# Dividing local probabilities before they are turned, instead of scaling the attention output by turned inverses

## The chip, the cores and the metric

The kernel runs on one core of a Trainium2 chip. The metric is the device time of one execution in microseconds. Before the change the median of three runs is 2158.35 us (2157.47 to 2159.66). The engines named below are PE (TensorE: matrix products and transposes), ACT (ScalarE), DVE (VectorE), POOL (GpSimd) and SP (the engine that issues most DMAs). Each takes its instructions strictly in program order and waits on semaphores where another engine has to be first.

## The reference, cut to what matters

The input is four sequences of 1024 tokens with 256 features. A first sublayer is causal attention with 16 heads of 16 features. The second part, in which the change lies, is two layers of local attention with a gated feed-forward, over the same four sequences:

```python
for l in range(2):                        # 8 heads of 64 features, windows of 128 tokens
    h = shift_token(x)
    q, k, v = split(h @ wqkv)
    q = l2norm(q) * q_scale ; k = l2norm(k) * k_scale
    q, k = rotary_xpos(q, k)
    # window w of queries looks at the keys of windows w-1 and w
    sim  = einsum('bhwid,bhwjd->bhwij', q * 8, k)        # 128 queries x 256 keys
    sim  = where(mask, -big, sim)
    attn = softmax(sim, axis=-1)
    x = x + einsum('bhwij,bhwjd->bhwid', attn, v) @ wo
    h = layernorm(shift_token(x)) * ln_g + ln_b
    a, g = split(h @ w1 + b1)
    x = x + (a * gelu(g)) @ w2 + b2
```

The softmax is exp(sim - max) divided by its sum over the keys. The sum belongs to one query of one head, so the division may be made on the 256 probabilities of each query and head, or after the product with v, on its 64 output features.

## The kernel before, in words

The block `layers` takes from about 740 us to the end. It runs eight iterations, `it` = 0 to 7: one layer of one sequence each, four for layer 0 and four for layer 1. An iteration is `attention(it)` and then `feed_forward(it, more)`, which also makes the first windows of the next iteration. The order on each engine is written out by hand.

`attention` counts steps u = 0 to 31 and some more. A window `w` = u // 4 has 128 tokens (`NT` = 8 windows), and a unit u is one window and two of its eight heads; `p` = u % 4. A unit goes through these stations:

- PE `scores` (L1414) writes the scores of two units, u and u+1 for even u, to the PSUM banks `s_ps`.
- DVE `mask_scores` (L1948) adds the band, takes the maximum and writes to `p_sb`, four operations of 128x256 for two units. `p_sb` is a ring of four units.
- ACT `exponentials` (L1680), two operations per unit, makes the exponentials in place in `p_sb` and leaves their sums in `total`. In step u stands unit u.
- PE `turn_probs` (L1485) transposes unit u-2 in step u into `pt_ps`, ACT `copy_probs` (L1702) copies it out, PE `values` (L1510) multiplies two units by v into `o_ps`.
- ACT `copy_output` (L1718) copies a finished window from `o_ps` to `o_t`, where features stand in the partitions and tokens in the free dimension.

The probabilities in `p_sb` are not normalised. DVE inverts the eight sums of a window in `invert_sums` (L2000). ACT spreads each inverse over 64 columns into `inv_wide` in `widen_sums` (L1711). PE transposes that with four transposes in `spread_sums` (L1494) into the bank `turn_ps`. DVE multiplies `o_t` by it in `scale_output` (L2006), and then `project_out` (L1430) may use it.

Between these stand the stations that prepare later windows, in the same queues. For window w+3: PE `project` (L1368), ACT `square` (L1643), DVE `sums` (L1919, at p = 3), POOL `norms` (a clamp, L1831, and a power, L1833). For window w+2: DVE `unit_vectors` (L1925, at p = 0) multiplies q and k by the inverse norms, DVE `times_sin` (L1939, at p = 1, four operations of 128x256) and POOL `rotate` (L1841 twice, then the addition L1846) turn them. DVE `low_x` (L1913, at p = 2) and ACT `high_x` (L1657) split the input of window w+4. PE `turn` (L1394) transposes q and k of window w+1 into `turn_ps`, ACT copies them out (L1672). `unit_vectors` and `times_sin` run for window indices w = 1 to 5, so five times in the `attention` of an iteration; `sums` runs there for w = 0 to 4.

In the trace `p_sb`, `qn`, `rot_c`, `squares`, `inv_wide` and `gate` are all called x_all, since they lie in that tile's memory.

## Time and profile before

| what | before |
|---|---|
| median of three runs | 2158.35 us |
| the profiled execution: its own time | 2157.21 us |
| its span | 2155.4 us |
| PE busy | 1973.2 us (92%) |
| DVE busy | 1466.5 us (68%) |
| ACT busy | 1260.7 us (58%) |
| POOL busy | 756.0 us (35%) |
| PE clock granted, mean share of full speed | 0.972 |

The profiled execution takes 1.8 us more than its span, and 1.1 us less than the median of the runs. The share of an engine's busy time is a mean over stages with quite different limits. The stretch of the change repeats in every iteration, so it is read from the order of time within one iteration.

### The profile page before, as it was taken

To read this page: it belongs to the slowest core of one execution; us is meant where nothing else is said; L and a number is where in the kernel's file an instruction comes from. 1 tells how busy PE (TensorE), PEld (TensorE's weight loads), DVE (VectorE), ACT (ScalarE), POOL (GpSimd) and SP (SyncE) were. 2 spreads that over 40 slices of the span, in tenths; PEclk is the share of its full clock that TensorE was granted. 3 is DMA by queue.
4 is the path that set the end of the run, shared out by engine and by line. 5 is a ranking of instruction groups with operands and counts; after the bars stand their busy time and mean duration, and the time that the engine had idled before them with its cause. 6 is when DMAs were issued, how large, how long until landed. Compare 5 with 4: busy or idle time off the path is not lost.

```text
span 2155.4 us, 36296 instructions
## 1 busy us (share of the span) xinstructions
PE 1973.2 (92%) x12096; PEld 1247.4 (58%) x12096; DVE 1466.5 (68%) x3928; ACT 1260.7 (58%) x3012; POOL 756.0 (35%) x631
## 2 busy tenths in 40 slices
PE   7978999999897669999999999999999999999998
PEld 4522333333234446777777676676777677777766
DVE  7778888888863557568568567557757756856854
ACT  4526666666664337647547646645755764754763
POOL 1033121121322456056046136236515605614610
PEclk9969999999999879999999999999999999999999
DMA  6667534535315620000000000023001000000000
GB/s 182 165 115 148 68 47 61 69 53 93 72 59 144 183 83 1 21 20 1 21 15 6 21 11 11 4 78 113 2 20 40 2 21 30 11 21 21 21 1 30
DMA packets 105335, 112.21 MB, mean 52 GB/s; under 512 B 49772, under 2 KB 84160, under 8 KB 104128
## 3 DMA queue, kind: packets, MB, share of 16 engines
q1 hardware_dynamic: 104576, 100.97, 20.6%
q0 software_dynamic: 576, 8.91, 1.1%
q8 instruction: 100, 1.64, 0.3%
q14 instruction: 83, 0.68, 0.1%
HBM read 67.12 MB, written 42.47 MB: 51 GB/s over the span
## 4 chain that ended last, share of the span: by engine, by line
PE 47%; DVE 6%; ACT 5%; issue 3%; POOL 3%; DVEq 0%; ACTq 0%; POOLq 0%
PE qkv_ps L1368 11%; PE s_ps L1414 5%; PE pt_ps L1485 5%; PE s_ps L1472 4%; PE o_ps L1510 3%; PE qkv_ps L1430 3%; PE pt_ps L1555 3%; POOL inv_norm L1833 2%; PE o_ps L1472 2%; PE pt_ps L1472 2%; PE s_ps L1430 2%; PE o_ps L1555 2%; ACT x_all L1680 2%; PE turn_ps L1394 2%; PE turn_ps L1494 1%
## 5 line engine op out<-in xcount | busy, mean ns | idle before, releaser
L689 ACT ACTIVATE probs<-st_ps 128x512 f32<-128x512 f32 (+3 forms) x768 | 330.0, 495 | 165.5 <-PE st_ps L594 164.9
L1368 PE MATMUL qkv_ps<-w_qkv,x_parts 128*128 128x512 f32 x1152 | 311.8, 415 | 25.6 <-DVE x_all L1925 18.8
L579 PE MATMUL s_ps<-k_stack,q_stack 96*128 96x512 bf16 (+3 forms) x768 | 242.6, 347 | 36.5 <-DVE piece_negmax L734 25.6
L734 DVE CUSTOM_DVE_ANT_0 att_in<-s_ps,causal 128x128 f32<-128x128 f32 (+3 forms) x512 | 233.7, 484 | 42.1 <-PE s_ps L579 41.9
L1368 PEld LDWEIGHTS qkv_ps<-w_qkv,x_parts 128*128 128x128 f32 x1152 | 214.3, 195 | 79.9 <-issue 30.0
L1680 ACT ACTIVATE x_all<-x_all,negmax 128x256 f32<-128x256 f32 (+1 forms) x512 | 249.4, 491 | 8.2 <-DVE negmax L1948 7.8
L1948 DVE CUSTOM_DVE_ANT_0 x_all<-s_ps,band 128x256 f32<-128x256 f32 (+1 forms) x512 | 178.3, 402 | 110.5 <-PE s_ps L1414 110.0
L594 PE MATMUL st_ps<-q_stack,k_stack 98*128 98x512 bf16 (+3 forms) x768 | 241.2, 335 | 12.3 <-ACT probs L689 10.1
L1702 ACT COPY att_in<-pt_ps 128x512 f32<-128x512 f32 (+1 forms) x256 | 143.0, 559 | 147.3 <-PE pt_ps L1485 145.9
L816 POOL TENSOR_SCALAR_AFFINE_SELECT probs<-probs 128x512 f32<-128x512 f32 x128 | 81.2, 634 | 414.7 <-ACT probs L689 414.7
L1841 POOL TENSOR_TENSOR x_all<-x_all,turn_by 128x512 f32<-128x512 f32 x128 | 179.9, 1425 | 101.4 <-PE turn_ps L1394 56.4
L1939 DVE TENSOR_TENSOR rot_s<-x_all,turn_by 128x256 f32<-128x256 f32 x256 | 207.3, 870 | 0.3
L737 DVE TENSOR_REDUCE piece_negmax<-s_ps 128x1 f32<-128x512 f32 x256 | 175.9, 687 | 29.3 <-PE s_ps L579 28.9
L1833 POOL TENSOR_TENSOR inv_norm<-sum_sq,neg_half 128x16 f32<-128x16 f32 x64 | 187.5, 2930 | 5.3
L1846 POOL TENSOR_TENSOR x_all<-x_all,rot_s 128x1024 f32<-128x1024 f32 x64 | 157.1, 2455 | 48.6 <-DVE rot_s L1939 48.5
L611 PE MATMUL o_ps<-probs,v_all 128*32 128x512 f32 (+3 forms) x1536 | 166.1, 505 | 1.2 <-POOL probs L816 0.7
L1485 PE MATMUL pt_ps<-ident,x_all 128*128 128x128 f32 x960 | 160.5, 287 | 6.9 <-ACT att_in L1702 6.9
L594 PEld LDWEIGHTS st_ps<-q_stack,k_stack 98*128 98x128 bf16 x768 | 72.1, 98 | 159.4 <-ACT probs L689 124.4
L579 PEld LDWEIGHTS s_ps<-k_stack,q_stack 96*128 96x128 bf16 x768 | 75.7, 99 | 149.4 <-DVE piece_negmax L734 71.4
L1414 PE MATMUL s_ps<-k_t,q_t 64*128 64x256 f32 (+1 forms) x1152 | 139.9, 366 | 0.8 <-DVE negmax L1948 0.8
L1485 PEld LDWEIGHTS pt_ps<-ident,x_all 128*128 128x128 f32 x960 | 101.4, 141 | 66.4 <-issue 59.3
L1472 PE MATMUL s_ps<-hn_t,w_ffn 128*128 128x512 f32 (+1 forms) x528 | 133.5, 400 | 0.0
(148 smaller groups left out, 3410.6 us busy)
## 6 DMA issues: line engine op xcount, KB each, us to landing
qk_scratch<-parts SPq DMA_DIRECT2D x64, 192.0 KB, 2.8
q_stack<-qk_scratch SPq DMA_DIRECT2D x96, 128.0 KB, 6.5
k_stack<-qk_scratch SPq DMA_DIRECT2D x96, 128.0 KB, 7.0
w_ffn<-ffn_weights POOLq DMA_DIRECT2D x4, 2176.0 KB, 11.5
x_in<-xt_scratch SPq DMA_DIRECT2D x16, 512.0 KB, 4.1
ffn_weights<-w_high SPq DMA_DIRECT2D x2, 2176.0 KB, 7.5
ffn_weights<-w_raw SPq DMA_DIRECT2D x2, 2176.0 KB, 13.1
att_scratch<-att SPq DMA_DIRECT2D x32, 128.0 KB, 2.0
```

What stands on the lines that cost most here:

```text
L579: pe.matmul(s_ps[i % 3][:, 0:kw], q_stack[0:STK, slot, h, qt * P:(qt + 1) * P], k_stack[0:STK, slot, h, k0:k0 + kw], start=True, stop=True ...
L594: pe.matmul(st_ps[i % 3][:, q0:CH], k_stack[0:STK + SHIFT, slot, h, kt * P:(kt + 1) * P], q_stack[0:STK + SHIFT, slot, h, c * CH + q0:(c + ...
L689: act.activation(probs[:, n % 3, h, q0:CH], st_ps[i % 3][:, q0:CH], ACT.Exp).then_inc(exp_done.sem, 1)
L734: dve.tensor_tensor_reduce(seen[:, i % 3, 0:kw], s_ps[i % 3][:, 0:kw], causal[:, CH - kw:CH], -1.0, BIG, ALU.add, ALU.min, result).then_in ...
L1368: mm = pe.matmul(qkv_ps[:, part * CH:(part + 1) * CH], x_parts[:, w % XR, xp, k, :], w_qkv[:, wp, k, part * INNER:(part + 1) * INNER], sta ...
L1414: mm = pe.matmul(s_ps[side][:, to:to + (t1 - t0) * P], q_t[r, w % 2, p, :], k_t[r, p, t0 % KR * P:(t0 % KR + t1 - t0) * P], start=True, st ...
L1472: mm = pe.matmul(up_pair(c, j)[bank][0:rows, :], w_up(w, k, tile)[:, 0:rows], hn_t[:, h, k, :], start=n == 0, stop=n == len(steps) - 1)
L1485: mm = pe.transpose(pt_ps[:, (h * 2 + kt) * P:(h * 2 + kt + 1) * P], p_sb[:, u % 4, h, kt * P:(kt + 1) * P], ident[:, :])
L1680: act.activation(p_sb[:, u % 4, h, k0:PW], p_sb[:, u % 4, h, k0:PW], ACT.Exp, scale=-1.0, bias=negmax[:, u % 4, h:h + 1], accum_out=total[ ...
L1833: pool.tensor_tensor(inv_norm[:, :], sum_sq[:, 1, :], neg_half[:, 0:2 * H2], ALU.pow)\
L1841: ins = pool.tensor_tensor(heads(rot_c, j), heads(qn, j), turn_by[:, w, 2 * j, :].unsqueeze(1) .to_broadcast([P, H2, HD2]), ALU.mult)
L1939: dve.tensor_tensor(dst[:, :, o], src[:, :, i], turn_by[:, w, 2 * j + 1, o].unsqueeze(1) .to_broadcast([P, H2, half]), ALU.mult).then_inc( ...
```

## The change

The probabilities of a unit are normalised before they are transposed. DVE gets a function `divide(u)`: a reciprocal of the unit's two sums (128x2) and a multiplication of the unit's probabilities in `p_sb` (128x512, 128x256 in window 0) by it, in place. The second waits for the first by a semaphore. At the end of each odd step DVE divides units u-1 and u. `turn_probs` waits for the division instead of the exponentials. `invert_sums`, `widen_sums`, `spread_sums` and `scale_output` are gone with their semaphores, and `project_out` waits for `copy_output` alone. ACT makes the exponentials of two units in succession in the even step, four operations, where it made two in each step. `total` and `inv_total` are a ring of four units.

```diff
-        total = sb("total", [P, 2, PAIRS, 2])
-        inv_total = sb("inv_total", [P, 2, PAIRS, 2])
+        total = sb("total", [P, 4, 2])
+        inv_total = sb("inv_total", [P, 4, 2])
...
-        inv_sum = count("inv_sum", NT, 2)
-        widened = count("widened", NT)
-        spread = count("spread", NT)
-        o_scaled = count("o_scaled", NT)
+        inv_sum = count("inv_sum", UNITS)
+        divided = count("divided", UNITS)
...
-                if w >= 3 and j == 0:
-                    pe.wait_ge(o_scaled.sem, o_scaled.of(it, w - 3))
...
-                pe.wait_ge(o_scaled.sem, o_scaled.of(it, t1 // P - 1))
+                pe.wait_ge(o_copied.sem, o_copied.of(it, t1 // P - 1))
...
-                    pe.wait_ge(exp_done.sem, exp_done.of(it, 2 * u + 1))
+                    pe.wait_ge(divided.sem, divided.of(it, u))
...
-                def spread_sums(w):
-                    pe.wait_ge(widened.sem, widened.of(it, w))
-                    pe.wait_ge(turn_copied.sem, turn_copied.of(it, 2 * min(w + 2, NT - 1) + 1))
-                    for p in range(PAIRS):
-                        mm = pe.transpose(turn_ps[:, p * P:(p + 1) * P], inv_wide[:, 2 * p:2 * p + 2, :], ident[:, :])
-                    mm.then_inc(spread.sem, 1)
...
-                    if u >= PAIRS + 2 and (u - 2) % PAIRS == 0:
-                        spread_sums((u - 2) // PAIRS - 1)
...
             def exponentials(it, u):
                 w, k0 = u // PAIRS, 0 if u // PAIRS else WIN
-                if u % PAIRS == 0:
-                    act.wait_ge(inv_sum.sem, inv_sum.of(it, w - 2))
                 for h in range(2):
                     act.wait_ge(s_masked.sem, s_masked.of(it, 2 * u + h))
                     act.activation(p_sb[:, u % 4, h, k0:PW], p_sb[:, u % 4, h, k0:PW], ACT.Exp, scale=-1.0,
                                    bias=negmax[:, u % 4, h:h + 1],
-                                   accum_out=total[:, w % 2, place(u, h)[0], place(u, h)[1]:place(u, h)[1] + 1]).then_inc(exp_done.sem, 1)
+                                   accum_out=total[:, u % 4, h:h + 1]).then_inc(exp_done.sem, 1)
...
-                def widen_sums(w):
-                    act.wait_ge(inv_sum.sem, inv_sum.of(it, w))
-                    if w:
-                        act.wait_ge(spread.sem, spread.of(it, w - 1))
-                    act.copy(inv_wide[:, :, :], inv_total[:, w % 2].rearrange("p a s -> p (a s)").unsqueeze(2)
-                             .to_broadcast([P, H2, HD2])).then_inc(widened.sem, 1)
...
-                    if EARLY <= u < UNITS:
+                    if EARLY <= u < UNITS and u % 2 == 0:
                         exponentials(it, u)
+                        exponentials(it, u + 1)
...
-                    if u >= PAIRS + 1 and (u - 1) % PAIRS == 0:
-                        widen_sums((u - 1) // PAIRS - 1)
...
-                def invert_sums(w):
-                    dve.wait_ge(exp_done.sem, exp_done.of(it, 2 * (w + 1) * PAIRS - 1))
-                    if w >= 2:
-                        dve.wait_ge(widened.sem, widened.of(it, w - 2))
-                    dve.reciprocal(inv_total[:, w % 2], total[:, w % 2]).then_inc(inv_sum.sem, 1)
-                def scale_output(w):
-                    dve.wait_ge(spread.sem, spread.of(it, w))
-                    dve.wait_ge(o_copied.sem, o_copied.of(it, w))
-                    window = o_t[:, :, w % WPC * P:(w % WPC + 1) * P]
-                    dve.tensor_tensor(window, turn_ps[:, :].rearrange("p (h t) -> p h t", h=PAIRS), window, ALU.mult)\
-                       .then_inc(o_scaled.sem, 1)
+                def divide(u):
+                    k0 = 0 if u // PAIRS else WIN
+                    dve.wait_ge(exp_done.sem, exp_done.of(it, 2 * u + 1))
+                    dve.reciprocal(inv_total[:, u % 4], total[:, u % 4]).then_inc(inv_sum.sem, 1)
+                    dve.wait_ge(inv_sum.sem, inv_sum.of(it, u))
+                    probs = p_sb[:, u % 4, :, k0:PW]
+                    dve.tensor_tensor(probs, probs, inv_total[:, u % 4, :].unsqueeze(2).to_broadcast([P, 2, PW - k0]),
+                                      ALU.mult).then_inc(divided.sem, 1)
...
-                    if u >= PAIRS + 1 and (u - 1) % PAIRS == 0:
-                        invert_sums((u - 1) // PAIRS - 1)
-                    if u >= PAIRS + 3 and (u - 3) % PAIRS == 0:
-                        scale_output((u - 3) // PAIRS - 1)
...
                     if p == 1 and 0 < w < NT - 2:
                         times_sin(it, w + 2)
+                    if u % 2 and u < UNITS:
+                        divide(u - 1)
+                        divide(u)
```

The first engine is DVE, at the place where `unit_vectors` and `times_sin` of a window stand (steps p = 0 and 1), before and after the change. An ISA row with x_all and s_ps is a mask operation, the ISA row behind it is the read-out of its maximum.

```order
L1925 TENSOR_TENSOR x_all<-qkv_ps,inv_norm 128x1024
L2000 RECIPROCAL inv_total<-total 128x8
L1939 TENSOR_TENSOR rot_s<-x_all,turn_by 128x8x32 x4
L1948 ISA x_all,negmax<-s_ps,band 128x256
L1948 ISA negmax 128x1
```

```order
L1899 TENSOR_TENSOR x_all<-qkv_ps,inv_norm 128x1024
L1913 TENSOR_TENSOR rot_s<-x_all,turn_by 128x8x32 x4
L1973 RECIPROCAL inv_total<-total 128x2
L1976 TENSOR_TENSOR x_all<-x_all,inv_total 128x512
L1973 RECIPROCAL inv_total<-total 128x2
L1976 TENSOR_TENSOR x_all<-x_all,inv_total 128x512
L1922 ISA x_all,negmax2<-s2_ps0,band 128x256
L1922 ISA negmax2 128x1
```

Two divisions now stand between `times_sin` and the masks of the next two units.

The next place on DVE is the end of the same window (p = 2 and 3), from `low_x` to the masks that follow, before and after.

```order
L1913 TENSOR_TENSOR x_parts<-x_in,x_parts 128x256
L1919 TENSOR_REDUCE sum_sq<-x_all 128x16
L2006 TENSOR_TENSOR o_t<-turn_ps,o_t 128x4x128
L1948 ISA x_all,negmax<-s_ps,band 128x256
L1948 ISA negmax 128x1
```

```order
L1887 TENSOR_TENSOR x_parts<-x_in,x_parts 128x256
L1893 TENSOR_REDUCE sum_sq<-x_all 128x16
L1973 RECIPROCAL inv_total<-total 128x2
L1976 TENSOR_TENSOR x_all<-x_all,inv_total 128x512
L1973 RECIPROCAL inv_total<-total 128x2
L1976 TENSOR_TENSOR x_all<-x_all,inv_total 128x512
L1922 ISA x_all,negmax2<-s2_ps0,band 128x256
L1922 ISA negmax2 128x1
```

The scaling of the output is gone and two divisions stand behind `sums`.

On ACT, from `copy_probs` at p = 2 to the next `copy_probs` but one; the ACTIVATE rows into x_all and total are the exponentials, the one from qkv_ps is `square`.

```order
L1702 COPY att_in<-pt_ps 128x512
L1680 ACTIVATE x_all,total<-x_all,negmax 128x256 x2
L1643 ACTIVATE x_all<-qkv_ps 128x1024
L1718 COPY o_t<-o_ps 128x4x128
L1702 COPY att_in<-pt_ps 128x512
L1680 ACTIVATE x_all,total<-x_all,negmax 128x256 x2
```

```order
L1685 COPY att_in<-pt_ps 128x512
L1663 ACTIVATE x_all,total<-x_all,negmax 128x256 x4
L1628 ACTIVATE x_all<-qkv_ps 128x1024
L1693 COPY o_t<-o_ps 128x4x128
L1685 COPY att_in<-pt_ps 128x512
L1650 COPY v_tok<-qkv_ps 128x512
```

`square` now stands behind four exponentials instead of two.

## Rows read from the trace of the kernel before

**Rows 1.** The page, busy time, share of the span and instructions of each engine.
```profile
PE 1973.2 (92%) x12096; PEld 1247.4 (58%) x12096; DVE 1466.5 (68%) x3928; ACT 1260.7 (58%) x3012; POOL 756.0 (35%) x631
```
**Rows 2.** Stretches: length, busy PE, PEld, DVE, ACT, POOL (instructions), granted clock, DMA.
```profile
1140.00:1189.50 49.50, 47.44 (x376) 35.79 (x376) 42.28 (x100) 38.33 (x102) 33.55 (x20) 1.00 0.01 2
...
690.00:700.00 10.00, 6.79 (x37) 4.98 (x38) 6.01 (x23) 2.68 (x9) 3.94 (x10) 1.00 0.88 265
...
750.00:760.00 10.00, 0.00 (x0) 0.00 (x0) 5.57 (x7) 0.46 (x1) 7.17 (x5) 0.73 0.00 0
760.00:770.00 10.00, 7.90 (x26) 6.25 (x26) 0.00 (x0) 2.15 (x3) 1.28 (x1) 0.58 0.01 2
```
**Rows 3.** Timeline of DVE, fourth iteration: start, duration, line, operands, [idle before].
```profile
1152.34 1.23 DVE L1925 TENSOR_TENSOR x_all<-qkv_ps,inv_norm 128x1024 f32<-128x1024 f32 x1 [0.30 <-POOL inv_norm L1833]
1153.48 0.19 DVE L2000 RECIPROCAL inv_total<-total 128x8 f32<-128x8 f32 x1
1153.60 3.61 DVE L1939 TENSOR_TENSOR rot_s<-x_all,turn_by 128x256 f32<-128x256 f32 x4
1157.13 0.41 DVE L1948 CUSTOM_DVE_ANT_0 x_all<-s_ps,band 128x256 f32<-128x256 f32 x1
...
1158.50 1.52 DVE L1913 TENSOR_TENSOR x_parts<-x_in,x_parts 128x256 fp32r<-128x256 f32 x1
1159.95 1.21 DVE L1919 TENSOR_REDUCE sum_sq<-x_all 128x16 f32<-128x1024 f32 x1
...
1164.65 1.23 DVE L1925 TENSOR_TENSOR x_all<-qkv_ps,inv_norm 128x1024 f32<-128x1024 f32 x1
...
1189.45 1.22 DVE L1925 TENSOR_TENSOR x_all<-qkv_ps,inv_norm 128x1024 f32<-128x1024 f32 x1
```
**Rows 4.** Timeline of POOL in the same window.
```profile
1157.35 2.39 POOL L1846 TENSOR_TENSOR x_all<-x_all,rot_s 128x1024 f32<-128x1024 f32 x1 [0.76 <-DVE rot_s L1939]
1161.35 0.25 POOL L1831 TENSOR_SCALAR sum_sq<-sum_sq 128x16 f32<-128x16 f32 x1 [1.61 <-DVE sum_sq L1919]
1161.68 2.93 POOL L1833 TENSOR_TENSOR inv_norm<-sum_sq,neg_half 128x16 f32<-128x16 f32 x1
```
**Rows 5.** Groups of instructions by line: shapes and count | busy us, mean ns.
```profile
L1494 PE MATMUL turn_ps<-ident,x_all 128*128 128x128 f32 x256 | 38.9, 274 | 4.5 <-ACT x_all L1711 4.5
L1711 ACT COPY x_all<-inv_total 128x512 f32<-128x512 f32 x64 | 39.6, 618 | 1.4 <-DVE inv_total L2000 1.0
L2006 DVE TENSOR_TENSOR o_t<-turn_ps,o_t 128x512 f32<-128x512 f32 x64 | 43.9, 685 | 91.4 <-ACT o_t L1718 91.4
```
**Rows 6.** Timeline of DVE in the causal part: a reciprocal and the multiplication that waits for it.
```profile
166.69 0.26 DVE L759 RECIPROCAL inv_sum<-ot_ps 128x16 f32<-128x16 f32 x1 [0.64 <-PE ot_ps L619]
166.98 0.42 DVE L762 TENSOR_TENSOR att<-ot_ps,inv_sum 128x256 f32<-128x256 f32 x1
```
**Rows 7.** Timeline of DVE and POOL in a feed-forward.
```profile
1278.07 1.21 DVE L1919 TENSOR_REDUCE sum_sq<-x_all 128x16 f32<-128x1024 f32 x1
1279.20 0.68 DVE L2048 TENSOR_TENSOR hidden<-x_all,hidden 128x512 fp32r<-128x512 f32 x1
1279.48 0.51 POOL L1831 TENSOR_SCALAR sum_sq<-sum_sq 128x16 f32<-128x16 f32 x1 [7.35 <-DVE sum_sq L1919]
1280.08 2.93 POOL L1833 TENSOR_TENSOR inv_norm<-sum_sq,neg_half 128x16 f32<-128x16 f32 x1
...
1281.31 0.41 DVE L1913 TENSOR_TENSOR x_parts<-x_in,x_parts 128x256 fp32r<-128x256 f32 x1
```
**Rows 8.** Timeline of ACT in the window of rows 3.
```profile
1157.58 0.51 ACT L1680 ACTIVATE x_all<-x_all,negmax 128x256 f32<-128x256 f32 x1
...
1158.86 1.02 ACT L1643 ACTIVATE x_all<-qkv_ps 128x1024 f32<-128x1024 f32 x1 [0.19 <-PE qkv_ps L1368]
```
**Rows 9.** Timeline of PE at the end of the attention.
```profile
1225.96 0.60 PE L1494 MATMUL turn_ps<-ident,x_all 128*128 128x128 f32 x4
```
**Rows 10.** Timeline of POOL in window 0 of the iteration.
```profile
1132.20 2.40 POOL L1846 TENSOR_TENSOR x_all<-x_all,rot_s 128x1024 f32<-128x1024 f32 x1 [0.76 <-DVE rot_s L1939]
```

More of the change, by code:

```diff
@@ L1148, in layers @@
         spare = x_all[:, :, :].rearrange("p t d -> p (t d)")
-        at = list(itertools.accumulate((0, GS * CH, 8 * PW, TC * D, H2 * HD2, 2 * INNER, 2 * INNER, 2 * INNER)))
-        gate, p_sb, fin, inv_wide, squares, qn, rot_c = [spare[:, i:j] for i, j in zip(at, at[1:])]
+        at = list(itertools.accumulate((0, GS * CH, 8 * PW, TC * D, 2 * INNER, 2 * INNER, 2 * INNER)))
+        gate, p_sb, fin, squares, qn, rot_c = [spare[:, i:j] for i, j in zip(at, at[1:])]
         gate = gate.rearrange("p (j n) -> p j n", j=GS)
@@ L1153, in layers @@
         fin = fin.rearrange("p (t d) -> p t d", t=TC)
-        inv_wide = inv_wide.rearrange("p (h d) -> p h d", h=H2)
         p_t = out_in[0][:, :, :, :].rearrange("p t g n -> p (t g n)").rearrange("p (u h k t) -> p u h k t", u=4, h=2, k=2)
@@ L1897, in _ @@
         def _(dve):
-            for c in (qn_ready, sin_ready, s_masked, inv_sum, mid_ready, hn_t_split, hidden_ready, hidden_split, out_ready):
+            for c in (qn_ready, sin_ready, s_masked, mid_ready, hn_t_split, hidden_ready, hidden_split, out_ready):
                 dve.sem_inc(c.sem, c.credit)
```

## The prediction

> **What bounds the kernel now.** I read the page's busy times first. PE is busy 92% of the span [rows 1], which suggests that whatever unloads PE helps. That is a mean, so I then took the busy times of the stretch that the change touches, 1140 to 1189.5 us, in the fourth iteration. There PE is busy for 47.4 of 49.5 us, but DVE too for 42.3 us [rows 2]. A busy PE is not PE at its peak, so the busy shares don't say who sets the pace. The order of time does [rows 3, 4]. One window, from one `unit_vectors` (L1925) to the next, takes 1164.65 - 1152.34 = 12.31 us, and no step of it is a wait for PE:
>
> - `unit_vectors` and the small reciprocal: 1152.34 to 1153.60, 1.26 us
> - `times_sin`: to 1157.13, 3.53 us
> - four masks: to 1158.50, 1.37 us
> - `low_x`: to 1159.95, 1.45 us
> - from the start of `sums` to the next `unit_vectors` 4.70 us: 1.21 us of `sums` and, behind it, POOL's clamp and its power of 2.93 us.
>
> Their sum is 12.31 us, the whole period. So the loop is closed by DVE and POOL: DVE is full from `unit_vectors` to the end of `sums`, and then POOL's power is waited for, while DVE does the scaling of the output and the next masks. The reader should see that work placed between `unit_vectors` and `sums` lengthens the window one for one, and that work placed behind `sums` is covered by POOL. The three periods from 1152.34 to 1189.45 have a mean of 12.37 us [rows 3]. Five `unit_vectors` stand in the attention of an iteration, with four periods between them, and with eight iterations there are 32 periods.
>
> **What goes.** 256 transposes on PE, 64 copies on ACT, 64 multiplications on DVE, of 38.9, 39.6 and 43.9 us busy [rows 5]. Four transposes occupy PE for at most 0.60 us [rows 9]. In the loop above none of this lies on the path; only the small reciprocal does, with 1.26 - 1.14 = 0.12 us a window (1152.34 to 1153.48 is 1.14). The 91.4 us in which DVE waits for ACT's copy of the output [rows 5] look like a prize, but most of them lie where DVE has no other work due (windows 6 and 7), so I count them at nothing.
>
> **What comes.** 256 reciprocals and 256 multiplications on DVE. The pair costs: a reciprocal of eight columns 0.19 us [rows 3]; between a reciprocal and a multiplication that waits for it by a semaphore 166.98 - 166.69 - 0.26 = 0.03 us [rows 6]; and a multiplication of 128x512 with both inputs in SBUF about 0.68 us, of which 0.61 before the next starts (the nearest row is L2048 [rows 7]). Two divisions are 2 x 0.83 = 1.66 us if nothing disturbs them.
>
> Something does, at the place behind `times_sin`. POOL's addition L1846 runs there from 1157.35 for 2.39 us, and `low_x`, a DVE operation with two SBUF inputs, took 1.52 us and ended 0.28 us after it [rows 3, 4]; the same operation takes 0.41 us where POOL does not do such work [rows 7]. The masks, with one input in PSUM, were not held up. In the other direction the clamp L1831 took 0.51 instead of 0.25 us beside L2048 [rows 4, 7]. I read this as: a two-input SBUF operation of DVE and a POOL operation take turns, whole. The Trainium skill (GPSIMD Engine Reference, Key points) says that GpSimd shares its SBUF interfaces with VectorE and contends with DVE instructions that have two SBUF inputs. By that rule the multiplications here, with two SBUF inputs, are the exposed kind and the scaling that goes, with one input in PSUM, was not; the trace agrees, 1.52 against 0.41 us. Without the rule the time would be that of the first rival below.
>
> So one of the two multiplications waits for most of L1846. If POOL is first (its addition starts 0.14 us after `times_sin` ended at 1157.21): 2.4 us, then 0.61, 0.22 and 0.61 us, 3.85 us in all. If DVE is first: 0.2 + 0.65 + 2.35 + 0.6 = 3.8. I take 3.8 us; the lower bound is 1.66 and the upper 1.66 + 2.39 = 4.05.
>
> **The new period.** Both divisions stand ahead of the masks, and the masks ahead of the exponentials, and `square` now stands behind four exponentials. Step by step from `unit_vectors`:
>
> - `unit_vectors` 1.14, `times_sin` 3.53, divisions 3.8
> - first mask to first exponential 1157.58 - 1157.13 = 0.45 [rows 3, 8]
> - four exponentials of 0.51 each [rows 8], 2.03
> - `square` to `sums`: 1159.95 - 1158.86 = 1.09. Until now `square` came early enough that DVE was the later one; now `sums` waits for it some 1.8 us, since masks and an unhindered `low_x` are over after 1.37 + 0.36 = 1.7 us against 3.57
> - `sums` to the next `unit_vectors` 4.70, and 0.45 more since the clamp meets the first multiplication of the divisions behind `sums`. In rows 7 that meeting moved the power to 2.01 us after the start of `sums`, against 1.73 (0.28 more); the new multiplication starts about 0.15 us later than L2048 did there.
>
> Sum 17.19 us against 12.37, so +4.82 us a period, 32 periods: +154.2 us. The divisions behind `sums` (1.66 us) and the next four masks (1.4 us) fit into the 3.9 us that POOL takes. PE needs at most 47.4 / 4 = 11.9 us a window (the stretch of rows 2 holds four periods) and gets 17, so it waits.
>
> **The rest of an iteration.** From the last `times_sin` to the end of the attention PE was nearly full. There four `spread_sums` of 0.6 us go, 2.4 us, and the scaling with its wait goes from the end. Against this stand a chain of about 4.2 us for two units (first mask to exponential 0.45, exponentials 2.03, divisions 1.66), below the 5 us that PE takes for two units there, and 3.8 us of divisions at its beginning. I estimate -0.5 us an iteration (bounds -2.5 and +3; the -2.4 nearly used up by the longer latency of each pair of units): -4 us. In window 0 the first division meets POOL's addition of 1132.20 to 1134.6 [rows 10], and `turn_probs` and `sums` come later: about +0.5 us (0 to 2): +4 us. The feed-forward is untouched.
>
> The total is 154.2 - 4 + 4 = +154 us. The profiled execution of 2157.2 us becomes 2311.4 us. The median of the runs lies 1.1 us higher than that execution, so I predict 2312 us, 7% slower.
>
> **Rivals.**
>
> - *No turn-taking for the divisions, or much overlap.* Then they cost 1.66 instead of 3.8 us behind `times_sin`: 2.14 x 32 = 68 us less, and without the late clamp another 0.45 x 32 = 14 us less, 2230 us. If `square` too were early enough, another 1.8 us a period, 2172 us would be the floor of this family. For it: `low_x` is the only such row in the loop. Against: the two rows agree in both directions.
> - *PE's clock falls.* PE now waits in each window, so its load drops to some 12 of 17 us. At 750 to 770 us, where PE did nothing for 10 us and then started again, the granted clock was 0.73 and 0.58, a mix of its two levels of 2.4 and 1.2 GHz; with PE busy for 6.8 of 10 us at 690 to 700 us it was 1.00 [rows 2]. The new waits are at most 3 to 4 us long, so I think it holds. If it halved in a third of the time, PE's 12 us a window would become 16, still below 17, and only the PE-bound stretches of about 40 us an iteration would pay, some 5 us each: 2350 us.
> - *Faster.* If PE is what sets the pace in the loop after all, 0.6 us of PE goes for each of 64 windows, 38 us, and DVE's divisions lie in its waits: 2119 us. It decides if the end of `sums` no longer sets the next `unit_vectors`, that is, if DVE had over 5 us of slack between them. The rows show 12.31 us of closed chain, so this is unlikely.
>
> **Chances.** The forecast's mechanism (2280 to 2335 us) 0.62; the milder cases (2172 to 2280) 0.22; the clock (2335 to 2400) 0.12; faster 0.02; another slow case 0.02. A measurement of this kernel can tell about 0.2% from no change. The range leaves out the far ends on either side: 2235 to 2345 us. Faster 0.02, within 0.2% 0.02, slower 0.96.
>
> **What the changed profile would show.** The period between two `unit_vectors` is 17 us (not 12.4); one of the two multiplications behind `times_sin` has a duration near 3 us, the others near 0.68; `sums` waits for ACT's `square`; `unit_vectors` still waits for POOL's power or starts right behind it; the clamp takes 0.5 to 0.7 us; PE has idle time of about 5 us a window, most of it ahead of L1485, released by DVE. The prediction is wrong if the multiplications behind `times_sin` are all short, if the loop is closed by another chain, or if the granted clock falls below 0.9 in the attention.

## The result, and the profile after

| | before | after |
|---|---|---|
| median of the runs | 2157.91 us (2156.68 to 2159.66, 4 runs) | 2339.18 us (2337.71 to 2340.73, 4 runs) |
| the profiled execution: own time | 2157.2 us | 2340.7 us |
| its span | 2155.4 us | 2339.0 us |
| PE clock granted, mean | 0.972 | 0.955 |

The change makes the kernel 8.35% slower: the ratio is 1.0835 [1.0822, 1.0848]. The prediction was 2312 us with a range of 2235 to 2345 us, so the direction and most of the size were right; 27 us were missing. The measured time lies 4 us above the 2280 to 2335 us that the prediction gave to its own mechanism.

The page of after, busy times, against [rows 1]:

```profile
PE 1993.8 (85%) x11840; PEld 1246.1 (53%) x11840; DVE 1668.8 (71%) x4312; ACT 1222.7 (52%) x2948; POOL 817.5 (35%) x631
```

PE lost 256 transposes and is busy 20 us longer all the same: the same matrix products took longer at a lower granted clock. DVE has 202 us more. POOL has the same 631 instructions and 61 us more, which only waiting inside them can explain.

One window of the loop, the timeline of DVE in after, fourth iteration, against [rows 3]. Of four masks (L1922) the first is shown, and of the four reciprocals (L1973, 0.15 us each) none:

```profile
1204.48 1.22 DVE L1899 TENSOR_TENSOR x_all<-qkv_ps,inv_norm 128x1024 f32<-128x1024 f32 x1 [1.45 <-POOL inv_norm L1807]
1205.74 3.59 DVE L1913 TENSOR_TENSOR rot_s<-x_all,turn_by 128x256 f32<-128x256 f32 x4
...
1209.44 0.69 DVE L1976 TENSOR_TENSOR x_all<-x_all,inv_total 128x512 f32<-128x512 f32 x1
...
1210.24 2.69 DVE L1976 TENSOR_TENSOR x_all<-x_all,inv_total 128x512 f32<-128x512 f32 x1
1212.84 0.41 DVE L1922 CUSTOM_DVE_ANT_0 x_all<-s_ps,band 128x256 f32<-128x256 f32 x1
...
1214.22 0.42 DVE L1887 TENSOR_TENSOR x_parts<-x_in,x_parts 128x256 fp32r<-128x256 f32 x1
1216.32 1.22 DVE L1893 TENSOR_REDUCE sum_sq<-x_all 128x16 f32<-128x1024 f32 x1 [1.68 <-ACT x_all L1628]
...
1217.64 0.69 DVE L1976 TENSOR_TENSOR x_all<-x_all,inv_total 128x512 f32<-128x512 f32 x1
...
1218.44 0.69 DVE L1976 TENSOR_TENSOR x_all<-x_all,inv_total 128x512 f32<-128x512 f32 x1
...
1221.95 1.23 DVE L1899 TENSOR_TENSOR x_all<-qkv_ps,inv_norm 128x1024 f32<-128x1024 f32 x1 [1.45 <-POOL inv_norm L1807]
```

POOL in the same window, against [rows 4]:

```profile
1209.47 2.89 POOL L1820 TENSOR_TENSOR x_all<-x_all,rot_s 128x1024 f32<-128x1024 f32 x1 [0.76 <-DVE rot_s L1913]
1217.73 0.71 POOL L1805 TENSOR_SCALAR sum_sq<-sum_sq 128x16 f32<-128x16 f32 x1 [5.37 <-DVE sum_sq L1893]
1218.53 3.39 POOL L1807 TENSOR_TENSOR inv_norm<-sum_sq,neg_half 128x16 f32<-128x16 f32 x1
```

ACT there, against [rows 8]; between the two rows stand the other three exponentials:

```profile
1213.30 0.51 ACT L1663 ACTIVATE x_all<-x_all,negmax 128x256 f32<-128x256 f32 x1 [1.83 <-DVE negmax L1922]
...
1215.28 1.00 ACT L1628 ACTIVATE x_all<-qkv_ps 128x1024 f32<-128x1024 f32 x1
```

The period is 1221.95 - 1204.48 = 17.47 us, where 17.19 was forecast. Of the two multiplications behind `times_sin` the second takes 2.69 us. It began at 1210.24 while POOL's addition ran from 1209.47 to 1212.36, and ended 0.57 us after that addition, about the length of one multiplication. The addition itself took 2.89 instead of 2.39 us, since the first multiplication, begun 0.03 us earlier, was ahead of it. `low_x` is down from 1.52 to 0.42 us, but `sums` waits 1.68 us for `square`.

In the last three iterations of after, the first of the four periods is shorter: 15.96, 15.11 and 15.11 us. Rows of DVE and POOL from the seventh, without the reciprocals:

```profile
1973.82 1.43 DVE L1913 TENSOR_TENSOR rot_s<-x_all,turn_by 128x256 f32<-128x256 f32 x4
1974.91 3.17 POOL L1815 TENSOR_TENSOR x_all<-x_all,turn_by 128x512 f32<-128x512 f32 x2 [2.38 <-PE turn_ps L1389]
...
1975.36 1.58 DVE L1976 TENSOR_TENSOR x_all<-x_all,inv_total 128x512 f32<-128x512 f32 x1
...
1977.05 1.57 DVE L1976 TENSOR_TENSOR x_all<-x_all,inv_total 128x512 f32<-128x512 f32 x1
```

Here POOL's own multiplications (L1815) came late, waiting for PE. `times_sin` took 1.43 us without them, where it takes 3.59 us beside them, and the two divisions met them instead. So `times_sin` takes turns with POOL too, and has done so before the change: its 3.61 us in [rows 3] lie beside POOL's L1841.

Adding up the starts of `unit_vectors` over all eight iterations tells where the 183.6 us of the two spans went. The loop is the time from the fourth to the eighth `unit_vectors` of an iteration (four periods), window 0 that from the first to the fourth, and the tail that from the eighth to the first of the next iteration:

| sums in us | before | after | difference | forecast |
|---|---|---|---|---|
| loop, 32 periods | 399.5 | 553.4 | +153.9 | +154.2 |
| window 0, 8 times | 371.5 | 376.4 | +4.9 | +4 |
| tails, 7 of them | 527.5 | 547.8 | +20.3 | -3.5 |
| behind the last `unit_vectors` | 102.9 | 107.3 | +4.4 | -0.5 |

(First and last starts 753.98 and 2052.51 us before, 754.10 and 2231.74 us after.) The loop is right and the tail is wrong. Stretches of whole tails, before first and then three of after: start and end, length, busy PE, PEld, DVE, ACT, POOL (instructions), granted clock, DMA; the third row of after is 4 us out of its second tail.

```profile
1189.45:1264.12 74.67, 71.25 (x441) 51.75 (x438) 39.25 (x107) 41.68 (x96) 11.03 (x9) 1.00 0.05 19
```

```profile
1064.07:1140.29 76.22, 68.79 (x415) 49.44 (x416) 47.73 (x121) 37.87 (x86) 12.66 (x9) 1.00 0.05 18
1256.94:1334.43 77.49, 70.88 (x419) 50.88 (x419) 47.63 (x121) 37.88 (x86) 12.66 (x9) 0.98 0.05 18
1284.92:1288.92 4.00, 4.00 (x27) 2.67 (x27) 1.77 (x8) 0.50 (x2) 0.00 (x0) 0.61 0.00 0
```

In the one tail of after that is at the full clock throughout PE is busy for 2.46 us less, as forecast (2.4 us), and yet the tail is 1.55 us longer: PE's idle time grew from 3.42 to 7.43 us. In six of the seven tails of after there are in addition between one and three stretches of some 4 us at 0.57 to 0.71 of the full clock, where six of seven tails of before were at 1.00 throughout. The same place on PE in before, the waits for DVE's `hn` and ACT's copy:

```profile
1215.74 1.09 PE L1449 MATMUL qkv_ps<-ident,hn 128*128 128x128 f32 x8 [1.26 <-DVE hn L1979]
...
1221.30 0.63 PE L1485 MATMUL pt_ps<-ident,x_all 128*128 128x128 f32 x4 [0.77 <-ACT att_in L1702]
```

and in after, in the tail that holds the third row above:

```profile
1279.48 0.63 PE L1480 MATMUL pt_ps<-ident,x_all 128*128 128x128 f32 x4 [1.02 <-ACT att_in L1685]
...
1284.06 1.46 PE L1444 MATMUL qkv_ps<-ident,hn 128*128 128x128 f32 x8 [2.35 <-DVE hn L1953]
1285.45 2.08 PE L1409 MATMUL s_ps<-k_t,q_t 64*128 64x256 f32 x8
...
1292.08 0.63 PE L1480 MATMUL pt_ps<-ident,x_all 128*128 128x128 f32 x4 [2.08 <-ACT att_in L1685]
```

The scores at 1285.45 take 2.08 us, at 1277.32 they took 1.14: the two levels of the clock, 1.2 and 2.4 GHz, behind a wait of 2.35 us for DVE.

### The profile page after: what moved, and what is told of

It is laid out like the page before. It is cut to its first block, busy times and chain, and to the rows that moved or that the text cites. A ratio compares the mean times of both kernels' runs of the same rounds, so it can differ in the third digit from the quotient of the medians.

```text
span 2339.0 us, 35807 instructions
## 1 busy us (share of the span) xinstructions
PE 1993.8 (85%) x11840; PEld 1246.1 (53%) x11840; DVE 1668.8 (71%) x4312; ACT 1222.7 (52%) x2948; POOL 817.5 (35%) x631
## 4 chain that ended last, share of the span: by engine, by line
PE 30%; DVE 16%; ACT 8%; POOL 8%; issue 6%; DVEq 0%; POOLq 0%; ACTq 0%
POOL inv_norm L1807 6%; DVE rot_s L1913 6%; PE qkv_ps L1365 4%; ACT x_all L1663 4%; PE s_ps L1467 4%; PE qkv_ps L1425 3%; PE pt_ps L1480 3%; DVE sum_sq L1893 3%; PE pt_ps L1540 2%; DVE x_all L1899 2%; PE s_ps L1409 2%; PE o_ps L1467 2%; PE pt_ps L1467 2%; PE o_ps L1540 2%; PE s_ps L1425 2%
## 5 line engine op out<-in xcount | busy, mean ns | idle before, releaser
L1480 PE MATMUL pt_ps<-ident,x_all 128*128 128x128 f32 x960 | 168.1, 297 | 141.3 <-DVE x_all L1976 116.7
L1976 DVE TENSOR_TENSOR x_all<-x_all,inv_total 128x512 f32<-128x512 f32 (+1 forms) x256 | 259.1, 1012 | 8.8
L1480 PEld LDWEIGHTS pt_ps<-ident,x_all 128*128 128x128 f32 x960 | 106.3, 146 | 210.8 <-DVE x_all L1976 176.6
L1815 POOL TENSOR_TENSOR x_all<-x_all,turn_by 128x512 f32<-128x512 f32 x128 | 183.6, 1453 | 93.3 <-DVE x_all L1899 68.9
L1922 DVE CUSTOM_DVE_ANT_0 x_all<-s_ps,band 128x256 f32<-128x256 f32 (+1 forms) x512 | 177.5, 400 | 39.1 <-PE s_ps L1409 36.2
L1807 POOL TENSOR_TENSOR inv_norm<-sum_sq,neg_half 128x16 f32<-128x16 f32 x64 | 203.4, 3178 | 5.3
L1913 DVE TENSOR_TENSOR rot_s<-x_all,turn_by 128x256 f32<-128x256 f32 x256 | 200.6, 843 | 1.7
L1820 POOL TENSOR_TENSOR x_all<-x_all,rot_s 128x1024 f32<-128x1024 f32 x64 | 177.2, 2768 | 54.3 <-DVE rot_s L1913 53.9
L1805 POOL TENSOR_SCALAR sum_sq<-sum_sq 128x16 f32<-128x16 f32 x64 | 33.4, 522 | 409.6 <-DVE sum_sq L1893 409.6
```

Source lines behind the costliest of these rows:

```text
L1480: mm = pe.transpose(pt_ps[:, (h * 2 + kt) * P:(h * 2 + kt + 1) * P], p_sb[:, u % 4, h, kt * P:(kt + 1) * P], ident[:, :])
L1807: pool.tensor_tensor(inv_norm[:, :], sum_sq[:, 1, :], neg_half[:, 0:2 * H2], ALU.pow)\
L1815: ins = pool.tensor_tensor(heads(rot_c, j), heads(qn, j), turn_by[:, w, 2 * j, :].unsqueeze(1) .to_broadcast([P, H2, HD2]), ALU.mult)
L1913: dve.tensor_tensor(dst[:, :, o], src[:, :, i], turn_by[:, w, 2 * j + 1, o].unsqueeze(1) .to_broadcast([P, H2, half]), ALU.mult).then_inc( ...
L1976: dve.tensor_tensor(probs, probs, inv_total[:, u % 4, :].unsqueeze(2).to_broadcast([P, 2, PW - k0]), ALU.mult).then_inc(divided.sem, 1)
```

## The experiments

All times are medians; the ratios are to the kernel before on the same chip. Four kernels change the changed kernel by one thing, then two take its multiplications away, one takes those of the tail alone, and three change the kernel before.

**a1: the exponentials of one unit in each step again.**

```diff
-                    if EARLY <= u < UNITS and u % 2 == 0:
+                    if EARLY <= u < UNITS:
                         exponentials(it, u)
-                        exponentials(it, u + 1)
```

> The changed kernel with the exponentials of one unit in each step again. Theory A (one closed chain: unit_vectors, times_sin, divisions held up by POOL's addition, first mask, exponentials, square, sums, POOL's power): square stands behind two exponentials instead of four, sums starts 1.0 us earlier after the first mask (2.5 instead of 3.5), the period falls from 17.5 to 16.5 us, 32 x 1.0 = 32 us, about 2307 us. Theory B (DVE is simply given 200 us more work, the order on the other engines does not matter): within 5 us of the 2339 us of the changed kernel.

Measured: 2316.56 us, ratio 1.0739 [1.0713, 1.0765], where theory A gave 2307 us. The period is 16.54 us, 0.94 less, and `sums` waits for `square` 0.70 instead of 1.68 us:

```profile
1210.15 1.22 DVE L1892 TENSOR_REDUCE sum_sq<-x_all 128x16 f32<-128x1024 f32 x1 [0.70 <-ACT x_all L1628]
```

So the four exponentials in succession cost what their place ahead of `square` says. The loop's sum fell by 24.6 us and not by 32, mainly because the last three iterations had a short first period already and gain only 1.5 to 2.3 us each; the tails' sum rose by 3.0 (a tail at the full clock takes 76.86 us), so undoing the pairs alone does not shorten the tail.

**a2: both divisions behind the next masks.**

```diff
                         mask_scores(it, u + 1)
+                    if u % 2 == 0 and 2 <= u < UNITS + 2:
+                        divide(u - 2)
+                        divide(u - 1)
...
-                    if u % 2 and u < UNITS:
-                        divide(u - 1)
-                        divide(u)
```

> The changed kernel with the two divisions moved behind the next four masks, the same instructions on every engine. Theory A: masks have an input in PSUM and run beside POOL's addition, the exponentials start right behind times_sin, and part of the addition is over when the first division comes; masks 1.4, divisions to 3.9, low_x to 4.3, then sums, so sums starts 4.3 us after times_sin instead of 7.1: period 14.7 us, about 2250 us. Theory B: the same work on DVE, no change, 2339 us.

Measured: 2590.27 us, ratio 1.2001 [1.1969, 1.2033], at a mean clock of 0.905. Both theories fail: they gave 2250 and 2339 us. Rows of DVE, ACT and PE in this kernel, in order of time, without the other masks, exponentials and reciprocals:

```profile
1308.61 0.42 DVE L1922 CUSTOM_DVE_ANT_0 x_all<-s_ps,band 128x256 f32<-128x256 f32 x1 [2.09 <-PE s_ps L1409]
...
1310.19 0.69 DVE L1976 TENSOR_TENSOR x_all<-x_all,inv_total 128x512 f32<-128x512 f32 x1
...
1310.93 1.07 PE L1480 MATMUL pt_ps<-ident,x_all 128*128 128x128 f32 x4 [2.62 <-DVE x_all L1976]
...
1312.04 0.59 ACT L1685 COPY att_in<-pt_ps 128x512 f32<-128x512 f32 x1 [4.19 <-PE pt_ps L1480]
1312.52 0.51 ACT L1663 ACTIVATE x_all<-x_all,negmax 128x256 f32<-128x256 f32 x1
...
1318.61 0.42 DVE L1922 CUSTOM_DVE_ANT_0 x_all<-s_ps,band 128x256 f32<-128x256 f32 x1 [4.33 <-PE s_ps L1409]
```

On ACT the exponentials of the new units stand behind `copy_probs` of the old ones. That copy needs PE's transposes, these need the division, and the division now stands behind the masks of the new units, which wait for PE's scores. So masks, division, transposes, copy and exponentials follow each other once for every two units (10.0 and 10.8 us, a period of 1329.38 - 1308.61 = 20.77 us), and PE, idle in between, is granted less clock. I had counted the busy time that moves and not what is queued behind each wait. The early place of the divisions, which the change has, is what keeps this chain open.

**a3: POOL's addition (L1820) over 16 of its 1024 columns.** It leaves out the rest of that addition.

```diff
-                pool.tensor_tensor(rot_c[:, :], rot_c[:, :], rot_s[:, :], ALU.add).then_inc(rot_ready.sem, 1)
+                pool.tensor_tensor(rot_c[:, 0:16], rot_c[:, 0:16], rot_s[:, 0:16], ALU.add).then_inc(rot_ready.sem, 1)
```

> The changed kernel, but POOL's addition in rotate covers 16 of 1024 columns (it leaves out the rest of the rotation, so its time is that of a kernel with less work on POOL). Theory A: the second multiplication behind times_sin takes 0.69 instead of 2.69 us, since it has no addition to wait for; the period falls by 2.0 us to 15.5 us, 32 x 2.0 = 64 us, about 2275 us. Rival C (a multiplication is slow there for another reason, such as ACT and PE reading the same memory): it stays near 2.7 us and the time within 10 us of 2339.

Measured: 2279.25 us (2273.69 to 2282.92), ratio 1.0558 [1.0524, 1.0593]. The second multiplication is down to 0.69 us and the period to 15.56 us:

```profile
1206.29 0.69 DVE L1976 TENSOR_TENSOR x_all<-x_all,inv_total 128x512 f32<-128x512 f32 x1
...
1207.09 0.69 DVE L1976 TENSOR_TENSOR x_all<-x_all,inv_total 128x512 f32<-128x512 f32 x1
```

The 2.0 us of the long multiplication are POOL's addition: 56.4 us of the loop's sum went with it, while the tails' sum rose by 4.4 us.

**a4: two operations with a per-partition scalar instead of one two-input multiplication.**

```diff
-                    probs = p_sb[:, u % 4, :, k0:PW]
-                    dve.tensor_tensor(probs, probs, inv_total[:, u % 4, :].unsqueeze(2).to_broadcast([P, 2, PW - k0]),
-                                      ALU.mult).then_inc(divided.sem, 1)
+                    for h in range(2):
+                        probs = p_sb[:, u % 4, h, k0:PW]
+                        ins = dve.tensor_scalar(probs, probs, inv_total[:, u % 4, h:h + 1], None, ALU.mult)
+                    ins.then_inc(divided.sem, 1)
```

> The changed kernel with each multiplication of 128x512 made as two tensor_scalar operations of 128x256, where the inverse sum is a scalar per partition instead of a second tensor from SBUF. Theory A with taking turns for two-tensor operations only: no wait for POOL's addition, 2 x 0.35 us a unit instead of 0.61 and one of them 2.6, so the period falls by 1.8 us to about 15.7 us, 58 us in 32 periods, and the power on POOL is no longer held up (0.4 us a period, 14 us): about 2268 us. Rival E (any DVE operation that reads and writes SBUF takes turns with POOL): one of the four is held up by 2 us as now, 2335 to 2345 us.

Measured: 2319.68 us, ratio 1.075 [1.0734, 1.0767]. DVE and POOL, from one window:

```profile
1203.96 2.39 POOL L1820 TENSOR_TENSOR x_all<-x_all,rot_s 128x1024 f32<-128x1024 f32 x1
...
1204.14 2.62 DVE L1977 TENSOR_SCALAR x_all<-x_all,inv_total 128x256 f32<-128x256 f32 x2
...
1211.48 0.62 DVE L1977 TENSOR_SCALAR x_all<-x_all,inv_total 128x256 f32<-128x256 f32 x2
```

The time lies between the 2268 us of theory A and the 2335 to 2345 us of rival E, but in kind E is right. With one large input, too, a pair of DVE operations takes 2.62 us beside POOL's addition and 0.62 us away from it. The pair ahead of it in this window took 2.65 us, beside POOL's multiplications (L1815), while `times_sin` took 1.43 us. "Two inputs in SBUF", as I had put it, is too narrow a condition. The Trainium skill (GPSIMD Engine Reference, Key points) names a second case beside that of two SBUF inputs, DVE instructions in a mode that uses both ports; these rows fit it, though no run here shows which mode they ran in. The pair is shorter than the one multiplication was (0.62 against 0.69 us), and POOL's addition is back at 2.39 us; the gain is 19.5 us, not the 71 us that theory A gave for freedom from POOL.

**a7: no multiplications; reciprocals, waits and order as in the change.** The probabilities stay without normalisation.

```diff
-                    dve.reciprocal(inv_total[:, u % 4], total[:, u % 4]).then_inc(inv_sum.sem, 1)
-                    dve.wait_ge(inv_sum.sem, inv_sum.of(it, u))
...
+                    dve.reciprocal(inv_total[:, u % 4], total[:, u % 4]).then_inc(divided.sem, 1)
```

> The changed kernel with the reciprocals and the order of everything, but without any of the 256 multiplications (the probabilities are not normalised). What is left is the new order alone. Theory A: from the end of times_sin 0.3 us of reciprocals, first mask 0.46, exponentials 1.98, square 1.04, sums to unit_vectors 4.70: period 13.3 us, 1 us more than before, since square stands behind four exponentials; 2157 + 32 us and the removed spread_sums in the rest of the iteration, 2175 to 2190 us. Theory B (cost is DVE's work): below the kernel before, near 2125 us, since DVE has less work than before.

Measured: 2214.90 us, ratio 1.0265 [1.0251, 1.0279], period 13.9 us, above what I expected. Rows of this kernel:

```profile
1160.49 0.40 DVE L1922 CUSTOM_DVE_ANT_0 x_all<-s_ps,band 128x256 f32<-128x256 f32 x1
...
1161.26 0.59 ACT L1685 COPY att_in<-pt_ps 128x512 f32<-128x512 f32 x1 [3.86 <-PE pt_ps L1480]
...
1161.74 0.51 ACT L1663 ACTIVATE x_all<-x_all,negmax 128x256 f32<-128x256 f32 x1
...
1164.76 1.22 DVE L1893 TENSOR_REDUCE sum_sq<-x_all 128x16 f32<-128x1024 f32 x1 [1.51 <-ACT x_all L1628]
```

The first exponential comes 1.25 us behind the first mask, not 0.45, because `copy_probs` stands ahead of it and waits for transposes that wait for the reciprocals. Of the 181 us, 57 are there without any multiplication and 124 come with them.

**a8: a7 with the exponentials of one unit in each step** (the edit of a1). It leaves out the normalisation as a7 does.

> The changed kernel without the multiplications (it leaves the normalisation out; turn_probs waits for the reciprocals of the two units), and with the exponentials of one unit in each step, as before the change. Theory A (of the 57 us that the order alone costs, the four exponentials in succession are the part in the loop): the period falls from 13.9 to about 12.96 us as it did by 0.94 us with the multiplications, 32 x 0.94 = 30 us, so 2185 us; the remaining 27 us lie outside the loop, in window 0 and the end of the attention. Theory H (the wait for the second unit's division holds up PE and ACT, whatever order the exponentials have): period stays near 13.9 us, 2210 to 2215 us.

Measured: 2181.03 us (2180.04 to 2188.69), ratio 1.012 [1.0102, 1.0138]; period 12.9 to 13.1 us. Of the 57 us of a7 the pairs are 34; 24 are left, 17.6 of them in the loop's sum and 8.9 in the tails', less 2.0 in window 0. So the time is as theory A had it, but not the place of what is left: it had put that outside the loop. Two of its tails with the same instructions:

```profile
849.94:925.96 76.02, 71.10 (x425) 50.97 (x420) 37.50 (x108) 39.71 (x92) 11.10 (x9) 0.98 0.05 18
1197.92:1272.69 74.77, 69.53 (x425) 49.92 (x420) 37.49 (x108) 39.52 (x92) 11.08 (x9) 1.00 0.05 19
```

One is at the full clock throughout and as long as in before (74.67). The other has one stretch of 4 us at 0.57 and is 1.25 us longer. In both, PE was busy for only 1.4 of the 4 us ahead of that place, waiting for DVE.

**a6: no multiplications for the units of windows 6 and 7.** It leaves their normalisation out.

```diff
                     dve.wait_ge(inv_sum.sem, inv_sum.of(it, u))
+                    if u >= 24:
+                        dve.sem_inc(divided.sem, 1)
+                        return
```

> The changed kernel without the multiplications of windows 6 and 7 (their probabilities are not normalised; the reciprocals and all waits stay), which leaves the closed chain of windows 1 to 5 as it is. The span from the last unit_vectors of an attention to the first of the next iteration is 3.1 us longer in the changed kernel than before. Theory F (the division's latency in the chain of two units lengthens it, since PE turns the last units only after it and the normalisation of tokens stands behind it on DVE): about 2 us an iteration come back, 2323 us. Rival G (PE's granted clock falls there because PE waited in the windows ahead, 0.70 and 0.77 in pieces of it): the span stays, less than 0.6 us an iteration, 2335 us or more.

Measured: 2328.19 us, ratio 1.0788 [1.0773, 1.0803]: 11 us less, between the two theories. A tail at the full clock:

```profile
1256.81:1331.80 74.99, 69.38 (x421) 49.85 (x420) 42.37 (x112) 38.14 (x86) 11.68 (x9) 1.00 0.05 18
```

It is 1.23 us shorter than that of after. Of the 11 us, 7.3 are in the seven tails, 2.6 behind the last `unit_vectors` and 3.2 in the loop's sum; window 0 and the part ahead of the first `unit_vectors` are 1.8 longer. Five of its seven tails still have a stretch of a lower clock.

**b1: the kernel before with POOL's addition over 16 columns.** It leaves out the rest of that addition, as a3.

> The kernel before with the same small POOL addition, a control (the same part of the rotation is left out). Theory A: low_x takes 0.41 instead of 1.52 us and stands on the closed chain, so the period of 12.3 us falls by up to 1.1 us, until PE with its 11.5 to 11.9 us a window sets it: 0.5 to 1.1 us a period, 16 to 35 us, 2122 to 2142 us. Rival D (PE sets the pace of the kernel before): no change, 2158 us.

Measured: 2149.93 us (10 runs), ratio 0.9963 [0.9951, 0.9975]. `low_x` fell from 1.52 to 0.42 us, but the period stayed at 12.3 us. The gain of 8 us is 2.5 us in the loop's sum and 5.9 us in window 0, so for the loop rival D is nearer:

```profile
1150.91 1.22 DVE L1925 TENSOR_TENSOR x_all<-qkv_ps,inv_norm 128x1024 f32<-128x1024 f32 x1 [0.29 <-POOL inv_norm L1833]
...
1157.06 0.42 DVE L1913 TENSOR_TENSOR x_parts<-x_in,x_parts 128x256 fp32r<-128x256 f32 x1
1158.49 1.22 DVE L1919 TENSOR_REDUCE sum_sq<-x_all 128x16 f32<-128x1024 f32 x1 [1.01 <-ACT x_all L1643]
...
1163.20 1.22 DVE L1925 TENSOR_TENSOR x_all<-qkv_ps,inv_norm 128x1024 f32<-128x1024 f32 x1
```

What DVE gained it waits for `square` now. The view that would have told me is the chain of waits of the kernel before, cut to two windows (1152 to 1178 us; start, length, what):

```profile
1152.96 0.63 PE turn_ps L1394 x4
1153.71 1.64 PE qkv_ps L1368 x6
1155.35 1.06 PE s_ps L1414 x8
1156.41 0.59 PE pt_ps L1485 x4
1157.00 0.44 PE turn_ps L1494 x4
```

It goes through PE nearly all the time. PE's own queue closes a second loop of the same length, beside that of DVE and POOL.

**b2: the kernel before with `low_x` behind `sums`**, away from POOL's addition.

```diff
-                    if p == 2 and w + AHEAD + 1 < NT:
-                        low_x(it, w + AHEAD + 1)
                     if p == 3 and w + AHEAD < NT:
                         sums(it, w + AHEAD)
+                    if p == 3 and w + AHEAD + 1 < NT:
+                        low_x(it, w + AHEAD + 1)
```

> The kernel before with low_x behind sums on DVE. In the run with the small POOL addition the period stayed 12.3 us though low_x fell to 0.42 us: sums then waited 1.0 us for square, which waits for PE's projection. Theory A with PE as a second limit of the same length: the period stays 12.3 us, only window 0 gains some tenths, 2150 to 2158 us. Rival H (the DVE and POOL chain alone sets the period): 1.1 us a period, 2123 us.

Measured: 2150.69 us (6 runs), ratio 0.9969 [0.9957, 0.998]. It is the fastest complete kernel here, by 0.3%. The loop's sum is 400.2 us (399.5 before), window 0's 365.6 (371.5): the gain is all in window 0, and the limit of PE holds in the loop, as b1 said.

**b3: the kernel before with the exponentials in pairs**, one part of the change alone (the edit of a1, reversed).

> The kernel before, with one part of the change alone: ACT makes the exponentials of two units in succession in each even step; the scaling of the output by turned inverses stays. Theory A (a square behind four exponentials makes the sums of squares late): from unit_vectors to the first mask 4.79 us, to the first exponential 0.45, four exponentials 2.03, square to sums 1.09, sums to the next unit_vectors 4.70, so a period of 13.06 us instead of 12.3, 32 x 0.75 = 24 us, 2182 us; if copy_probs stands in front of the first exponential as in the run with reciprocals only (first exponential 1.25 us behind the masks), up to 13.8 us and 2206 us. Theory H (in the kernel before this order costs nothing, since PE is as long as the loop of DVE and POOL and square has slack): 2158 us, period 12.3 us.

Measured: 2199.13 us, ratio 1.0197 [1.018, 1.0214], in the upper half of theory A. The loop's sum rises by 27.7 us (mean periods of 13.2 to 13.5 us by iteration) and the tails' by 12.1. A row of DVE:

```profile
1187.28 1.22 DVE L1920 TENSOR_REDUCE sum_sq<-x_all 128x16 f32<-128x1024 f32 x1 [0.91 <-ACT x_all L1643]
```

`low_x` is still held up here (1.54 us), so `sums` is late by both. The tails are at 76.4 us at the full clock. After, which has the pairs but not the turned inverses, has 76.2, and a7 75.1; so the 1.7 us here come from the pairs together with the chain over the turned inverses. PE's waits for ACT's copies are what grows: 1.16 us for `q_t` at the start of the tail instead of 0.18, and 0.58 and 1.64 us for `att_in` instead of one of 0.77.

## Why the prediction was right or wrong, point by point

- *DVE and POOL close the loop, so work between `unit_vectors` and `sums` counts in full.* Right for the changed kernel: its 32 periods give +153.9 us of +154.2. For the kernel before, the words "no step of it is a wait for PE" said too much: b1 shows a second limit of equal length. It did no harm, since a change that lengthens the one loop by 4.8 us leaves the other behind. The first rival's "`low_x` is the only such row in the loop" was wrong too: `times_sin`, 3.61 us beside POOL's multiplications and 1.43 us without them, is another, and speaks for taking turns.
- *Divisions and POOL's addition take turns: 3.8 us for the two.* Right in kind and size: 3.59 us, and a3 takes the 2.0 us away. a4 widens the condition on DVE's side; on POOL's side it is narrower than "a POOL operation", since `low_x` took its usual 0.41 us inside POOL's power [rows 7].
- *Four exponentials ahead of `square`.* 1.98 us and a wait of 1.68 us (forecast 2.03 and 1.8); undone in a1 for 0.94 us a period, and in the kernels without multiplications (a7, a8) for about 0.9.
- *From `sums` to `unit_vectors` 0.45 us later.* Too small: 5.63 us against 5.15. The clamp meets the first multiplication (0.71 instead of 0.25 us), and the power meets the second and takes 3.39 instead of 2.93 us. I had counted only the first meeting. That is 0.48 x 32 = 15 us. The other terms together came out 0.20 us shorter (the divisions 0.21, while the 0.12 us of the small reciprocal were not won: `times_sin` still starts 1.26 us behind `unit_vectors`), so the period is 0.28 us longer than forecast. That the loop's difference still came out right is partly luck: three iterations of after need less for their four periods (68.45, 67.6 and 67.6 instead of 69.96 us), and the 32 periods of before have a mean of 12.49 us where I took 12.37.
- *The tail: -0.5 us an iteration, bounds -2.5 and +3.* This is the step that failed: +24.7 us in all instead of -4, about 3.1 us an iteration. I had set a chain of 4.2 us for two units against the 5 us that PE takes for them, and concluded that PE stays full. PE did get its 2.4 us back, but was no longer fed: the waits of 1.26 us for `hn` and 0.77 us for the copy became 2.35 us (2.67 in the tail at the full clock), and 1.02 and 2.08 us. The copy stands behind four exponentials on ACT, `hn` behind two divisions on DVE; neither station was in my chain. At the full clock the tail is 1.55 us longer (12.4 us over eight iterations, if the one such tail of after stands for all). Of this a6 takes 1.23 us away, and the wait for `hn` falls there to 1.43 us while those for the copy stay at 1.01 and 2.08. The waits for the copy come of the pairs, as a8 has 0 and 1.10 us in their place; but a1 is no shorter at the full clock, so how the 1.55 us divide between the two parts stays open. The other 12 us or so are a remainder that I put down to the stretches at a lower clock; they are not a measured price. a8's two tails, equal but for the clock, price one such stretch at 1.25 us, but a1 has tails of 76.86 us with one (granted clock 0.98) and without (1.00). What brings the stretches on stays open. Before has none in six of seven tails, which points to the waits of PE; but a8 has the same waits in tails with and without one, and a4 has none in any of its seven tails, though PE is idle there for 8.3 us (76.88 - 68.61), more than the 7.43 us of after.
- *The rival of the clock, 2350 us.* The measured time lies in this rival's interval (2335 to 2400 us), which had a chance of 0.12, and not in the forecast's own. The clock fell to 0.88 in the loop as well (1186.98 to 1256.94 us), at no cost there, as PE had time to spare: the periods are 17.5 us as in loops at 0.96. What is this rival's is at most the 12 us above; the loop came by the forecast's mechanism. My sign that the prediction would be wrong if the clock fell below 0.9 in the attention was badly chosen: a low clock counts only where PE is the bound.
- *The change does what it says.* PE, ACT and DVE lost the work of [rows 5], and none of it showed as a gain: a8, which has lost all of it and adds only reciprocals and a wait, is 1.2% slower than before.

## What to carry to other kernels

Price a new instruction by its place: the same multiplication cost 0.69 us or 2.69 us, and each of the two placed behind `sums` delayed POOL's own chain. Before calling one engine's loop the bound, look at the chain of waits over one period as well; two loops can be equally long, and then a gain in one is worth nothing. In a stretch in which an engine is nearly full, work taken off it is no gain if the change also makes its inputs later: add up the latency of one unit from station to station beside the busy time.

## What the runs showed of the hardware

- A DVE operation with two inputs in SBUF that met POOL's addition or one of its multiplications waited until that instruction had ended: 0.69 became 2.69 us beside an addition of 128x1024 and 1.58 us beside L1815, and stayed 0.69 where the addition had 16 columns (a3). Masks, which read PSUM (0.41 us), and a reciprocal of 128x2 (0.16 us at 1210.05) went on beside the addition.
- Not every POOL instruction held DVE up: `low_x` took 0.41 us inside POOL's power [rows 7], 1.52 us beside its addition.
- DVE operations with one input in SBUF and a per-partition scalar were held up by the addition as well (a4), and it works the other way round: POOL's power of 128x16 took 3.39 instead of 2.93 us, its clamp 0.71 instead of 0.25 us.
- Equal instructions in one execution can run with and without a stretch of 4 us at the lower clock (a8), behind the same waits of PE; a4, with 8.3 us of idle PE in a tail, has no such stretch in any of seven tails.
